# Three dense attentions as one unrolled pipeline of slots, with some scaling moved to GpSimd

## The chip, the cores and the metric

The kernel runs on one core of a Trainium2 chip. The metric is the device time of one launch in microseconds; 2329.51 us is the median of three runs of the kernel before.

## The reference

Four transformer layers, each an attention and a feed-forward part, run on x of 2 x 256 tokens with 512 features; every part starts with a layer norm and adds its result to x. The change touches the attentions of the first three layers, the dense attentions:

```
L0: q = norm(x) Wq, k = ctx Wk, v = ctx Wv (32 heads of 128, 8 key heads; q and k rotated), 512 keys
L1: q = norm(x) Wq, k, v of [ctx, norm(x)]  (16 heads of 96, 4 key heads),  512 + 256 keys
L2: q = norm(x) Wq, k, v of [ctx, norm(x)]  (32 heads of 128, 4 key heads), 512 + 256 keys
x = x + softmax(q k^T * scale [+ mask]) v Wo
```

Float32 accuracy is kept by splitting every operand into a high and a low part (`hi`, `lo`); each product is three matmuls, hi*hi, lo*hi and hi*lo (`passes`, L297).

## The kernel before, in words

A dense attention goes through groups of four query heads: 8 groups in L0, 4 in L1, 8 in L2. One group has the four query heads' projections, the projection of keys and values (in L2 only every second group), 16 tiles of 128 queries by all keys, and the output projection. A tile is: scores on TensorE; the row maximum on VectorE; the exponential with row sum on ScalarE; the reciprocal on VectorE; the scaling, on ScalarE for even and on VectorE for odd tiles (L659, L759); the turn (transposes) on TensorE into a PSUM bank; the high half on ScalarE (L669) and the low half on VectorE (L777). In L1 and L2 the 768 keys of a tile are turned in two pieces, of 512 and 256 columns. Two tiles are a unit, and `attend` multiplies its turned probabilities with the values.

`body` writes one group (two for L2) and `loop` (L410) repeats it in a hardware loop. On TensorE a group is three stretches one after the other: the projections in, then the `PIPE` of 20 steps with the tiles (step i: scores of tile i, turn of tile i-2, at even i attend), then the output projections. The turned pieces p take the PSUM banks `ps_t[p % 3]`, and a turn waits only for the low half of the piece three before it:

```
if p >= 3:
    e.wait_ge(s_tlo, g * (TILES * len(l.pieces)) + (c.piece + p - 2))
```

VectorE in step i does the reciprocal of tile i-1, the low half of the attention's output, the maximum of tile i, the odd scaling, and the low half of tile i-2. In L0 the rotation of q and k (swap of halves on ScalarE L628, products with cosine and sine on VectorE L707 and L708, their sum on GpSimd L477, the halves by L640 and L389) stands ahead of the pipe, and the swap of job r+1 is issued before the sum of job r is waited for. GpSimd else splits the weights that SyncE's queue loads (`split`, L313).

Every engine's queue runs in the order in which it is written, and semaphore counts order the engines among each other. The feed-forward parts and the fourth attention are not touched but for names of PSUM banks.

Of the kernel before, what the change touches and what calls it, by code (L numbers as in the profile page):

```python
# [20 lines left out]
ALU = mybir.AluOpType  # L21
# [7 lines left out]
P = 128  # L29
B, SQ, SK, D = 2, 256, 512, 512  # L30
T = B * SQ
# [35 lines left out]
def program(nc, A, out):  # L67
    ctx = ExitStack()
    with ctx:
# [44 lines left out]
        def attention_space(l):  # L114
# [9 lines left out]
            s.q = [take("q_hi", [P, HG, T], F32R), take("q_lo", [P, HG, T], F32R)]  # L124
# [3 lines left out]
            s.ot = [take("ot_hi", [P, HG, T], F32R), take("ot_lo", [P, HG, T], F32R)]  # L128
# [86 lines left out]
        ps_s = [ctx.enter_context(nc.psum_tensor(f"ps_s{i}", [P, 2, 512], F32)) for i in range(2)]  # L215
# [3 lines left out]
        ring = [ps_s[0][:, 0, :], ps_s[0][:, 1, :], ps_s[1][:, 0, :], ps_s[1][:, 1, :]]  # L219
# [30 lines left out]
        s_go = sem("tile_taken")  # L250
        s_rot = sem("rotation_parts")
        s_swap = sem("halves_swapped")
        s_nat = [sem("even_rows_in"), sem("odd_rows_in")]
# [3 lines left out]
        class Start:  # L257
# [3 lines left out]
            def __init__(self, g, hi, tile, piece, unit, q, kv, o, ra):  # L261
                self.g, self.hi, self.tile, self.piece, self.unit = g, hi, tile, piece, unit
                self.q, self.kv, self.o, self.ra = q, kv, o, ra
        counts = {n: 0 for n in ("g", "hi", "tile", "piece", "unit", "q", "kv", "o", "ra")}
# [8 lines left out]
        def attention_counts(l):  # L273
            n = l.groups
            kv = n // l.kv_every
            phase(l.name, g=kv * l.kv_tiles + n * 8, hi=kv * l.kv_hi + n * HG, tile=n * TILES,
                  piece=n * TILES * len(l.pieces), unit=n * UNITS, q=n, kv=kv, o=n,
                  ra=n * (HG + 2) if l.rope else 0)
# [121 lines left out]

        class Attention:
            def __init__(self, l, A, first_before, free=None):

                self.free = free
                self.l, self.s, self.c = l, SP[l.name], START[l.name]
                self.wkv, self.wq, self.wo = A[l.name + "_wkv"], A[l.name + "_wq"], A[l.name + "_wo"]
                self.first_before = first_before
                self.per = l.kv_every

            def loop(self, e, body):  # L410

                n = self.l.groups // self.per
                with e.Fori(0, n - 1) as i:
                    body(e, i, False)
                body(e, n - 1, True)

            def q_start(self, it, s):

                return it * (self.l.kv_tiles + 8 * self.per) + (self.c.g + (self.l.kv_tiles + 8 * s if s else 0))  # L420

            def o_start(self, it, s):
                return it * (self.l.kv_tiles + 8 * self.per) + (self.c.g + self.l.kv_tiles + 8 * s + HG)

            def hi_start(self, it, s):
                return it * (self.l.kv_hi + HG * self.per) + (self.c.hi + (self.l.kv_hi + HG * s if s else 0))

            def grp(self, it, s):
                return it * self.per + s
# [7 lines left out]
            def sp(self, e):  # L437
                l, c = self.l, self.c

                def body(e, it, last):  # L440
                    for s in range(self.per):
                        g = self.grp(it, s)
                        load(e, "o", None, self.wo[g], ("q", g + (c.q + 1)), parts=l.hd)
                        if s == self.per - 1 and not last:
                            load(e, "kv", None, self.wkv[it + 1], ("kv", it + (c.kv + 1)), cols=2 * l.hd)
                        if not (last and s == self.per - 1):
                            load(e, "q", None, self.wq[g + 1], ("o", g + (c.o + 1)), cols=HG * l.hd)
                self.loop(e, body)
# [12 lines left out]
            def pool(self, e):  # L461
                l, c, sp = self.l, self.c, self.s

                def body(e, it, last):
                    for s in range(self.per):
                        g = self.grp(it, s)
                        q0, o0 = self.q_start(it, s), self.o_start(it, s)
                        more = [("o", g + c.o, q0, p, l.hd, 512) for p in range(4)]
                        if s == self.per - 1 and not last:
                            more += [("kv", it + (c.kv + 1), o0, p, P, 2 * l.hd) for p in range(4)]  # L470
                        if not (last and s == self.per - 1):
                            more += [("q", g + (c.q + 1), o0, p, P, HG * l.hd) for p in range(4)]
                        if l.rope:
                            ra0 = it * (HG + 2) + c.ra
                            for t in range(HG + B):
                                e.wait_ge(s_rot, ra0 * 2 + (2 * t + 2))
                                e.tensor_tensor(sp.ra[:, t % 2, :], sp.ra[:, t % 2, :], sp.rb[:, t % 2, :], ALU.add)\  # L477
                                    .then_inc(s_ra, 1)
                        for job in more:
                            split(e, *job)  # L480
                self.loop(e, body)

            def pe(self, e):
# [3 lines left out]
                def body(e, it, last):  # L488
                    def bank(n, q0):

                        e.wait_ge(g_free, q0 + (n - 3))
                        return ring[n % 4]
                    for s in range(self.per):
                        g = self.grp(it, s)
                        q0, o0 = self.q_start(it, s), self.o_start(it, s)

                        def project_in(o, role, c0, src, lo, first=False):

                            for d in range(DK):
                                if first:  # L500
                                    e.wait_ge(g_free, c.g - 3 + d)
                                    e.wait_ge(w_rdy["q"], g * 8 + (8 * c.q + 2 * d + 2))
                                mm = passes(e, o[0:hd, :], planes(W[role], slice(None), d, slice(c0, c0 + hd)),
                                            planes(src, slice(None), d, slice(lo, lo + 512)), d == 0, d == DK - 1)
                            mm.then_inc(g_full, 1)
                        for hh in range(HG if s == 0 else HG - 1):
                            project_in(bank(hh, q0), "q", hh * hd, xT, 0, hh == 0)
                        if s == 0:

                            e.wait_ge(w_rdy["kv"], it * 8 + (8 * c.kv + 8))  # L510
                            e.wait_ge(s_csplit, DK)
                            for n, (src, lo) in enumerate([(cT, b * SK) for b in range(B)] + ([(xT, 0)] if l.self_keys else []), HG):
                                project_in(bank(n, q0), "kv", 0, src, lo)
# [1327 lines left out]
```

## Time and profile before

| | us |
|---|---|
| median of 3 runs (lowest, highest) | 2329.51 (2327.69, 2330.35) |
| span of the profiled execution | 2328.4 |
| what lies around the span, against the median | 1.1 |
| TensorE matmul busy | 2063.1 (89%) |
| VectorE busy | 1558.6 (67%) |
| ScalarE busy | 1142.4 (49%) |
| GpSimd busy | 901.6 (39%) |
| DMA | 37 GB/s on average |

The profile gives the execution's own time as its span, from the first to the last instruction. A matmul's busy time is its modelled passage through the array, longer than the distance between two starts; where work per matmul is counted below, it is the distance from start to start.

### The profile page before, as it was taken

Reading aid. Unit: us, or ns where it says so; the run is one execution under the profiler, and the core shown is the slowest. Engines: PE = TensorE matmul, PEld = TensorE weight load, DVE = VectorE, ACT = ScalarE, POOL = GpSimd, SP = SyncE. Lnnn points to the kernel's source line nnn. Section 1 sums busy time; section 2 is a strip of 40 time slices with the busy share of each in tenths; the row PEclk is TensorE's granted clock in tenths of the full one; section 3 lists DMA queues with packets and bytes.
Section 4 is the critical chain, followed back from the end, with each engine's and each line's share of the span. In section 5 each row is a group of like instructions: output and inputs, shape, how many; then the busy total and the mean of one; then the engine's idle time right before and its main releaser. Section 6 shows DMA issues by size and latency. Waiting matters only on the chain. (4 is left out here: it accounts for less than half of the span.)

```text
span 2328.4 us, 34351 instructions
## 1 busy us (share of the span) xinstructions
PE 2063.1 (89%) x11612; PEld 1707.9 (73%) x11616; DVE 1558.6 (67%) x3108; ACT 1142.4 (49%) x2338; POOL 901.6 (39%) x850
## 2 busy tenths in 40 slices
PE   5989999899879999987999999999988899996667
PEld 4777777777658788786888888888876677775535
DVE  5677666776657466475764674576564695897999
ACT  3556455565316256351653563555540594782430
POOL 7355533554432322224141233222316674662612
PEclk9999999999989999998999999999999999998889
DMA  3111001110110001001010011001101101002301
GB/s 137 46 45 45 18 27 45 45 36 18 62 30 25 14 22 34 19 12 62 28 37 20 28 37 32 33 19 39 37 28 43 37 1 55 1 19 77 127 18 37
DMA packets 20011, 87.16 MB, mean 37 GB/s; under 512 B 2736, under 2 KB 8624, under 8 KB 11440
## 3 DMA queue, kind: packets, MB, share of 16 engines
q1 hardware_dynamic: 19888, 85.55, 10.6%
q8 instruction: 74, 1.21, 0.2%
q14 instruction: 49, 0.40, 0.1%
HBM read 84.49 MB, written 1.05 MB: 37 GB/s over the span
## 5 line engine op out<-in xcount | busy, mean ns | idle before, releaser
L777 DVE TENSOR_TENSOR l_pt_lo<-ps_t,l_pt_hi 128x512 fp32r<-128x512 f32 (+1 forms) x512 | 283.2, 584 | 87.3 <-ACT l_pt_hi L669 80.1
L323 POOL TENSOR_TENSOR wo_hi<-raw_big,one 128x512 fp32r<-128x512 f32 (+2 forms) x116 | 123.0, 1060 | 489.6 <-PE ps_s L301 460.0
L669 ACT ACTIVATE l_pt_hi<-ps_t 128x512 fp32r<-128x512 f32 (+1 forms) x512 | 243.8, 515 | 108.1 <-PE ps_t L563 103.8
L563 PE MATMUL ps_t<-ident,l_p 128*128 128x128 f32 x1664 | 244.8, 277 | 45.9 <-DVE l_pt_lo L777 29.4
L563 PEld LDWEIGHTS ps_t<-ident,l_p 128*128 128x128 f32 x1664 | 191.9, 141 | 84.3 <-DVE l_pt_lo L777 37.7
L299 PE MATMUL ps_o<-l_pt_hi,l_v_hi 128*128 128x256 f32 (+1 forms) x704 | 211.7, 301 | 14.3 <-DVE l_pt_lo L777 14.3
L323 POOL TENSOR_TENSOR wq_hi<-raw_big,one 128x512 fp32r<-128x512 f32 (+1 forms) x120 | 126.1, 1051 | 199.7 <-PE ps_o L529 98.2
L299 PE MATMUL ps_s<-l_k_hi,l_q_hi 128*128 128x512 f32 (+3 forms) x512 | 195.9, 383 | 7.7 <-DVE l_k_lo L387 3.9
L754 DVE TENSOR_REDUCE nmax<-ps_s 128x1 f32<-128x768 f32 x192 | 183.0, 953 | 28.6 <-PE ps_s L301 28.3
L301 PE MATMUL ps_o<-l_pt_hi,l_v_lo 128*128 128x256 f32 (+1 forms) x704 | 200.0, 284 | 0.0
L300 PE MATMUL ps_o<-l_pt_lo,l_v_hi 128*128 128x256 f32 (+1 forms) x704 | 199.9, 284 | 0.0
L681 ACT ACTIVATE l_p<-ps_s,nmax 128x768 f32<-128x768 f32 x192 | 173.6, 904 | 28.2 <-DVE nmax L754 28.2
L477 POOL TENSOR_TENSOR l_ra<-l_ra,l_rb 128x512 f32<-128x512 f32 x48 | 76.3, 1591 | 271.8 <-DVE l_rb L708 270.7
L300 PE MATMUL ps_s<-l_k_lo,l_q_hi 128*128 128x512 f32 (+3 forms) x512 | 180.8, 353 | 0.0
L301 PE MATMUL ps_s<-l_k_hi,l_q_lo 128*128 128x512 f32 (+3 forms) x512 | 180.6, 353 | 0.0
L1125 POOL TENSOR_TENSOR l_p<-l_p,rinv 128x512 f32<-128x512 f32 x128 | 132.3, 1040 | 84.1 <-DVE rinv L1295 84.1
L299 PE MATMUL ps_s<-xT_hi,wq_hi 128*128 128x512 f32 (+1 forms) x384 | 152.6, 397 | 10.5 <-issue 10.0
L325 POOL TENSOR_TENSOR wq_lo<-raw_big,wq_hi 128x512 fp32r<-128x512 f32 (+1 forms) x120 | 156.4, 1303 | 9.4
L325 POOL TENSOR_TENSOR wo_lo<-raw_big,wo_hi 128x512 fp32r<-128x512 f32 (+2 forms) x116 | 152.0, 1310 | 9.1
L659 ACT ACTIVATE l_p<-l_p,rinv 128x768 f32<-128x768 f32 (+1 forms) x160 | 135.9, 849 | 34.9 <-DVE rinv L735 34.5
L299 PEld LDWEIGHTS ps_o<-l_pt_hi,l_v_hi 128*128 128x128 f32 (+1 forms) x704 | 130.2, 185 | 29.4 <-DVE l_pt_lo L777 21.2
L300 PE MATMUL ps_s<-xT_lo,wq_hi 128*128 128x512 f32 (+1 forms) x384 | 151.1, 394 | 0.0
(309 smaller groups left out, 5552.1 us busy)
## 6 DMA issues: line engine op xcount, KB each, us to landing
raw_big<-in_l_wq SPq DMA_DIRECT2D x18, 1024.0 KB, 5.0
raw_big<-in_l_wo SPq DMA_DIRECT2D x18, 1024.0 KB, 4.9
raw_big<-in_f_w SPq DMA_DIRECT2D x10, 1024.0 KB, 5.0
raw_kv<-in_l_wkv SPq DMA_DIRECT2D x12, 512.0 KB, 5.7
q_nat<-in_f_w1n SPq DMA_DIRECT2D x4, 1024.0 KB, 4.8
q_nat<-in_f_w2n SPq DMA_DIRECT2D x4, 1024.0 KB, 4.8
raw_big<-in_l_wq SPq DMA_DIRECT2D x4, 768.0 KB, 4.7
raw_big<-in_l_wo SPq DMA_DIRECT2D x4, 768.0 KB, 5.5
```

Of the source, the lines that this page charges most:

```text
L299: pe.matmul(o, a[0], b[0], start=start, stop=False)
L300: pe.matmul(o, a[0], b[1], start=False, stop=False)
L301: return pe.matmul(o, a[1], b[0], start=False, stop=stop)
L323: pool.tensor_tensor(hi, w, one[0:parts, 0:1].to_broadcast([parts, cols]), ALU.mult).then_inc(w_rdy[role], 1)
L325: pool.tensor_tensor(lo, w, hi.bitcast(F32), ALU.subtract).then_inc(w_rdy[role], 1)
L563: mm = e.transpose(ps_t[p % 3][:, k * P:(k + 1) * P], sp.p[:, i % 3, (k0 + k) * P:(k0 + k + 1) * P], ident[:, :])
L659: e.activation(pr, pr, ACT.Copy, scale=rinv[:, i - 1:i]).then_inc(s_scl[0], 1)
L669: e.activation(sp.pt[u % 2][0][:, k0:k0 + nk, qt * P:(qt + 1) * P], ps_t[p % 3][:, 0:nk * P].rearrange("p (k q) -> p k q", q=P), ACT.Copy) ...
L681: e.activation(sp.p[:, i % 3, :], src, ACT.Exp, bias=nmax[:, i:i + 1], scale=-1.0 if l.rope else 1.0, accum_out=rsum[:, i:i + 1]).then_inc ...
L754: e.tensor_reduce(nmax[:, i:i + 1], ps_flat(i)[:, 0:l.keys], AX.X, ALU.max, negate=True).then_inc(s_max, 1)
L777: e.tensor_tensor(pt[1], ps_t[p % 3][:, 0:nk * P].rearrange("p (k q) -> p k q", q=P), pt[0].bitcast(F32), ALU.subtract).then_inc(s_tlo, 1)
L1125: e.tensor_tensor(l3p[:, i % 4, :], l3p[:, i % 4, :], rinv[:, i % TILES:i % TILES + 1].to_broadcast([P, SK]), ALU.mult).then_inc(s3["scl"], 1)
```

## The change

The hardware loops go; the attention is written out as one sequence of slots over all its tiles (`N` = 128, 64, 128), with six or eight slots ahead of tile 0 that hold one whole projection each and four behind. In slot k TensorE does scores of tile k, then parts of projections (a part is three matmuls, a quarter of a job), turned values, the turn of tile k-2, and at even k attend. `ORDER` spreads a group's jobs evenly over its 16 slots: q of the next group, o (the output projection) of the group before, k and v of the next; a capital letter is the part of the keys that comes from x (256 columns). L1 has 16 jobs a group, one per slot; L0 and L2 have 12, three parts per slot. Group 0 has no o jobs and the last group no q jobs and no k0, v0.

q has two buffers, and the attention's output is written into the q it came from. The projections use two PSUM banks in turn, ring[3] and ps_t[2]; the turned pieces therefore have two banks (before three), and attend one (before two in L0). In L1 and L2 the scores of odd and even tiles share a bank for their x keys. The odd tiles of L1 and L2 are scaled on GpSimd, between weight splits assigned to slots; in L0 they stay on VectorE.

```
 ORDER = {
   "l0": ["k1 o0 o1 v1 o2 o3 q0 k0 q1 v0 q2 q3"],
   "l1": ["k1 K1 o0 v1 V1 o1 o2 o3 q0 k0 K0 q1 v0 V0 q2 q3"],
   "l2": ["k1 K1 o0 v1 V1 o1 o2 o3 q0 q1 q2 q3", "o0 o1 o2 o3 q0 q1 k0 K0 q2 v0 V0 q3"]}
 FIRST = {"l0": "q0 q1 q2 q3 k0 v0", "l1": "q0 k0 K0 q1 v0 V0 q2 q3", "l2": "q0 k0 K0 q1 v0 V0 q2 q3"}
   # TensorE
+  def take_turn_bank(p):
+      if p >= 2:
+          e.wait_ge(s_tlo, c.piece + p - 1)
+      return ps_t[p % 2]
+  for k in self.slots:
+      if 0 <= k < self.N: scores(k)
+      for j, part in self.parts.get(k, ()): project(j, part)
+      for j in self.values.get(k, ()): turn_values(j)
+      if 0 <= k - 2 < self.N: turn(k - 2)
+      if self.unit_at(k) is not None: attend(self.unit_at(k))
   # inside scores(k)
+      if k >= 2: e.wait_ge(s_max if l.rope else s_exp, c.tile + k - 1)
...
+      if l.self_keys and k >= 1: e.wait_ge(s_exp, c.tile + k)     # ahead of the x keys
   # ScalarE, slot k
+      turned_hi(k - 3)                       # high halves of tile k-3
+      # high half of attend's output (odd k)
+      for j in self.ended.get(k - 1, ()):    # rotated jobs only
+          e.wait_ge(s_ra, j.rope + 1); e.activation(qk_tile hi, sp.ra)
+      e.wait_ge(s_max, ...); e.activation(... ACT.Exp ...)
+      # high half of turned values
+      for j in self.ended.get(k, ()):        # wait g_full: swap of halves (L0), or high half of q/k
+      if k % 2 == 0: e.wait_ge(s_rec, ...); e.activation(pr, pr, ACT.Copy, scale=rinv)
   # VectorE, slot k
+      largest(k)
+      turned_lo(k - 3)
+      # low half of attend's output (odd k)
+      # low half of the q/k rotated in slot k-1
+      # reciprocal of tile k
+      # low half of turned values
+      for j in self.ended.get(k, ()):        # rotate(j), or low half of q/k, or copy of v / x += o
+      if k % 2 == 1 and l.rope: tensor_scalar(pr, pr, rinv)
   # GpSimd, L1 and L2
+      if i % 2:
+          e.wait_ge(s_rec, c.tile + k + 1)
+          e.tensor_scalar(pr, pr, rinv[:, i:i + 1], None, ALU.mult).then_inc(s_scl[1], 1)
+      if 2 <= i < 6: next_q(g, i - 2)
+      if kv_at <= i < kv_at + 2: next_kv(g, 2 * (i - kv_at)); next_kv(g, 2 * (i - kv_at) + 1)
+      if o_at <= i < o_at + 4: own_o(g, i - o_at)
```

(A comment stands for a call whose operation is as in the kernel before.) SyncE's queue issues the same loads in the order q of the next group, kv, o.

## Rows read from the trace of the kernel before

**Rows 1.** Busy time by stretch: L0, L1, L2, then two groups of L2.
```profile
17.00:616.00 599.00, 540.63 (x2891) 441.50 (x2889) 396.77 (x861) 331.13 (x680) 285.32 (x248) 0.98 0.10 36
680.00:1041.00 361.00, 347.07 (x2080) 291.70 (x2079) 210.05 (x401) 178.01 (x364) 87.52 (x97) 0.98 0.09 24
1080.00:1731.00 651.00, 623.20 (x3808) 549.86 (x3808) 400.16 (x754) 340.51 (x700) 169.18 (x163) 0.99 0.09 31
1346.59:1506.96 160.37, 154.37 (x950) 136.02 (x949) 98.70 (x185) 84.45 (x174) 42.60 (x40) 1.00 0.09 31
```

**Rows 2.** Waits of the weight loads in L1: total us, times, longest.
```profile
PEld ps_t L563 <- DVE l_pt_lo L777: 11.3, 8, 1.8
PEld ps_o L529 <- DVE xn L766: 2.7, 4, 0.7
```

**Rows 3.** The same in L2.
```profile
PEld ps_t L563 <- DVE l_pt_lo L777: 26.4, 26, 2.0
...
PEld ps_s L299 <- DVE l_q_lo L389: 2.4, 4, 0.6
```

**Rows 4.** Timeline of TensorE in L2: start, duration, operation.
```profile
1366.37 0.82 PE L563 MATMUL ps_t<-ident,l_p 128*128 128x128 f32 x6
...
1371.61 0.40 PE L299 MATMUL ps_s<-l_k_hi,l_q_hi 128*128 128x512 f32 x1
1371.84 0.40 PE L300 MATMUL ps_s<-l_k_lo,l_q_hi 128*128 128x512 f32 x1
...
1372.66 0.60 PE L563 MATMUL ps_t<-ident,l_p 128*128 128x128 f32 x4
```

**Rows 5.** Timeline of L2: VectorE, and the turn that waits for it.
```profile
1368.29 1.02 DVE L777 TENSOR_TENSOR l_pt_lo<-ps_t,l_pt_hi 128x512 fp32r<-128x512 f32 x2 [0.30 <-ACT l_pt_hi L669]
...
1369.03 0.44 PE L563 MATMUL ps_t<-ident,l_p 128*128 128x128 f32 x2 [0.36 <-DVE l_pt_lo L777]
...
1369.54 0.96 DVE L754 TENSOR_REDUCE nmax<-ps_s 128x1 f32<-128x768 f32 x1
...
1370.41 0.61 DVE L759 TENSOR_SCALAR l_p<-l_p,rinv 128x768 f32<-128x768 f32 x1
...
1372.86 0.96 DVE L754 TENSOR_REDUCE nmax<-ps_s 128x1 f32<-128x768 f32 x1 [0.21 <-PE ps_s L301]
```

**Rows 6.** Timeline of L0: exponential, low half, attend.
```profile
216.12 0.71 ACT L681 ACTIVATE l_p<-l_p,nmax 128x512 f32<-128x512 f32 x1
...
216.26 0.69 DVE L777 TENSOR_TENSOR l_pt_lo<-ps_t,l_pt_hi 128x512 fp32r<-128x512 f32 x1 [0.19 <-ACT l_pt_hi L669]
...
217.01 0.39 PE L299 MATMUL ps_o<-l_pt_hi,l_v_hi 128*128 128x256 f32 x1 [0.28 <-DVE l_pt_lo L777]
```

**Rows 7.** Timeline of L0: one rotation.
```profile
181.97 1.21 ACT L628 ACTIVATE l_rb<-ps_s 64x512 f32<-64x512 f32 x2 [1.51 <-PE ps_s L301]
...
183.21 0.69 DVE L707 TENSOR_TENSOR l_ra<-ps_s,l_cos 128x512 f32<-128x512 f32 x1 [1.43 <-ACT l_rb L628]
...
184.58 1.67 POOL L477 TENSOR_TENSOR l_ra<-l_ra,l_rb 128x512 f32<-128x512 f32 x1 [1.43 <-DVE l_rb L708]
...
186.28 0.63 ACT L640 ACTIVATE l_q_hi<-l_ra 128x512 fp32r<-128x512 f32 x1 [0.38 <-POOL l_ra L477]
```

**Rows 8.** Timeline of L0: rotations at its start, first scores, last projection.
```profile
37.74 0.63 ACT L640 ACTIVATE l_q_hi<-l_ra 128x512 fp32r<-128x512 f32 x1 [11.86 <-POOL l_ra L477]
...
52.59 0.50 PE L299 MATMUL ps_s<-l_k_hi,l_q_hi 128*128 128x512 f32 x1 [0.48 <-DVE l_k_lo L387]
...
611.38 0.39 PE L299 MATMUL ps_s<-wo_hi,l_ot_hi 128*128 128x512 f32 x1
...
612.51 0.39 PE L301 MATMUL ps_s<-wo_hi,l_ot_lo 128*128 128x512 f32 x1
```

**Rows 9.** Page, costliest groups: scaling of 512 columns on GpSimd, fourth attention.
```profile
L1125 POOL TENSOR_TENSOR l_p<-l_p,rinv 128x512 f32<-128x512 f32 x128 | 132.3, 1040 | 84.1 <-DVE rinv L1295 84.1
```

**Rows 10.** Page, DMA queues: instructions.
```profile
q8 instruction: 74, 1.21, 0.2%
```

More of the change, by code:

```diff
@@ L123, in take @@
                 return a
-            s.q = [take("q_hi", [P, HG, T], F32R), take("q_lo", [P, HG, T], F32R)]
+            s.q = [[take(f"q{i}_{n}", [P, HG, T], F32R) for n in ("hi", "lo")] for i in range(2)]
             s.k = [take("k_hi", [P, B, l.keys], F32R), take("k_lo", [P, B, l.keys], F32R)]
@@ L438, in sp @@
                 l, c = self.l, self.c
[L440 to L448, printed above, removed]
+                for g in range(l.groups):
+                    before = self.raw_before(g)
+                    if g + 1 < l.groups:
+                        load(e, "q", None, self.wq[g + 1], before, cols=HG * l.hd)
+                        before = ("q", c.q + g + 2)
+                    kv = g // l.kv_every
+                    if g % l.kv_every == 0 and kv + 1 < self.kvs:
+                        load(e, "kv", None, self.wkv[kv + 1], ("kv", c.kv + kv + 1), cols=2 * l.hd)
+                    load(e, "o", None, self.wo[g], before, parts=l.hd)
             def pool_first(self, e):
@@ L462, in pool @@
                 l, c, sp = self.l, self.c, self.s
[L464 to L480, printed above, removed]
@@ L481, in pool, with next_q, next_kv @@
-                self.loop(e, body)
+                def next_q(g, piece):
+                    if g + 1 < l.groups:
+                        split(e, "q", c.q + g + 1, self.full(self.find["q", g, 3, False]), piece, cols=HG * l.hd)
+                def next_kv(g, piece):
+                    kv = g // l.kv_every
+                    if g % l.kv_every == 0 and kv + 1 < self.kvs:
+                        split(e, "kv", c.kv + kv + 1, self.full(self.find["v", kv, 1, l.self_keys]), piece, cols=2 * l.hd)
@@ L617, in act @@
+                for k in self.slots:
+                    if 0 <= k < self.N:
+                        scores(k)
+                    for j, part in self.parts.get(k, ()):
+                        project(j, part)
+                    for j in self.values.get(k, ()):
+                        turn_values(j)
+                    if 0 <= k - 2 < self.N:
+                        turn(k - 2)
+                    if self.unit_at(k) is not None:
+                        attend(self.unit_at(k))
             def act(self, e):
@@ new lines, in project_out @@
+                def project_out(j):
+                    e.wait_ge(g_full, self.full(j))
+                    if j.kind == "v":
+                        if j.stage >= 4:
+                            old = [v for v in self.jobs if v.stage == j.stage - 4][0]
+                            e.wait_ge(s_T, c.piece + self.v_piece[old.n] + 1)
+                        e.tensor_copy(xn[0:hd, j.stage % 4, 0:j.width], self.bank(j)[0:hd, 0:j.width]).then_inc(g_free, 1)
+                        return
+                    t = j.i
+                    if j.g:
+                        e.wait_ge(g_free, self.full(self.find["o", j.g - 1, t, False]))
+                    e.tensor_tensor(x[:, t, :], self.bank(j), x[:, t, :], ALU.add).then_inc(g_free, 1)
+                    if j.g == l.groups - 1 and t < TT - 1:
+                        e.wait_ge(g_free, self.full(j))
+                        e.bn_stats(st[:, t, :], x[:, t, :])
```

655 lines of the change are left out of this document (340 added, 315 removed), and 3 rows, old and new, of the table ORDER.

## The prediction

> **What bounds the kernel now.** First the busy time by stretch [rows 1]: in the three dense attentions (599, 361 and 651 us) TensorE's matmuls are busy for 540.6, 347.1 and 623.2 us, at a granted clock of 0.98 to 0.99, while VectorE has 397, 210 and 400. TensorE bounds all three. A busy time overstates a pipelined matmul, so I count from start to start. In the timeline of L2 [rows 4] a matmul of 512 columns takes 1371.84 - 1371.61 = 0.23 us (0.227 over the five steps between the last two starts of [rows 8]), one of 256 columns 0.12, the scores of a tile with 768 keys 1372.66 - 1371.61 = 1.05, six transposes 0.65 and four 0.44 (0.109 each; the six start at 1366.37 and take 0.82 to their modelled end). In these units the work is: L0 a group, twelve jobs of 12 x 0.227 = 2.72, 16 scores of 0.70, 16 turns of 0.44, 8 attends of 12 x 0.12 = 1.44, turned values 0.9: 63.3 us. L1 84, two groups of L2 together 150.8. In all 505, 337 and 602 us, so that 94, 24 and 49 us are not work. That is all that an ideal pipeline could win, 167 us.
>
> Second the waits of the weight loads, which show a gap as it is from start to start: L1 11.3 us behind the low half of the turned pieces and 2.7 behind the values [rows 2]; L2 26.4 and 2.4 [rows 3] and again 2.7 behind the values (word for word the row of [rows 2]). The rest of L1 and L2 (10 and 17 us) is the end of the attention up to the next norm and rounding of my units; it stays.
>
> **The change, L1 and L2.** What goes: 14.0 and 31.5 us of waits [rows 2, 3]. What comes is one wait for every slot. With two banks in place of three, the first piece of tile k-2 may be turned only when the low half of the first piece of tile k-3 is done, and VectorE does that in the same slot k, behind the maximum of tile k, which waits for the scores of slot k. The rows price it [rows 5, 4]: scores end (1372.66) to maximum 0.20; maximum to VectorE's next operation 1370.41 - 1369.54 = 0.87; start of a low half to the turn that it releases 1369.03 - 1368.29 = 0.74. So the turn of slot k starts no earlier than 1.81 us after its scores, that is 2.86 into the slot. Between them lie only the projection parts, and what decides is whether they last 1.81:
> - Full slots do: three parts 2.04 (L2), a job 2.72 (L1). No stall. VectorE's last operation, the low half of a job, ends at 4.6 (1.05 + 2.04 + 0.2 + 0.64 for the high half + 0.61), in an odd slot of 3.74 that is 0.9 into the next, whose maximum starts at 1.25.
> - A slot with a K or V job has 1.44 in L1, 1.40 in L2: 0.4 us.
> - A slot without a job: 1.81.
> - Where values are turned too, the second piece of tile k-2 waits for their low half, which on VectorE stands behind the reciprocal and on ScalarE behind the exponential: values turned to 3.3, high half 3.5 to 4.1, low half visible at 4.87. That is 1.5 us in a slot with a short job, 0.6 behind a full one, 2.3 where there is no job.
>
> L1: group 0 lacks its four o jobs (three plain 1.81, one 2.4 with values: 7.8) and has 0.4 + 1.5 + 1.5 + 0.6 for the others: 11.8. Groups 1 and 2 have 0.4 x 2 + 1.5 x 2 + 0.6 x 2 = 4.9 each. Group 3 has eight slots without a job, 14.5, and 2.5 for its first half: 17.0. The last turns, without a maximum between, wait for high and low half in turn: 2. Sum 40.6.
> L2: group 0 lacks 16 of 48 parts: 12.7. The six groups between: three short slots at 0.4, values 1.55 and 0.6: 3.4 each, 20.4. Group 7 lacks 32 parts: ten slots at 1.81 and one at 1.1, 19.2. End 2. Sum 54.3.
> Net: L1 40.6 - 14.0 = +26.6; L2 54.3 - 31.5 = +22.8.
>
> **The scaling on GpSimd.** The nearest row is the fourth attention's, 1.04 us for 512 columns [rows 9]; 768 columns of one operand lie between 1.04 and, by width, 1.56; I take 1.56, the cautious one. The reciprocal is there at 3.5 in slot k, the turn starts at 3.1 in slot k+2, in all 9.2 us later. Beside it stand at most two pieces of split, 2.3 each, queued behind it and not ahead of it. If it took twice 1.56 the turn would still find it done. VectorE is relieved of 0.61 to 1.7 us every second tile, but it is not what bounds. Zero, from 0 to +3 us.
>
> **L0.** Its tiles have one piece, so the two banks cost nothing: low half of tile k-3 is needed by attend, at 0.70 + 2.04 + 0.44 = 3.18 in an even slot; without a delay it is there at 0.9 + 0.65 + 0.74 = 2.3 (low half to attend 217.01 - 216.26 = 0.75 [rows 6]). The delay comes from the rotation. In slot k ScalarE waits for the sum of the job that ended in slot k-1 ahead of the exponential, and swaps the halves of slot k's job behind it; VectorE rotates behind that, ahead of the next maximum. So successive rotated jobs form a circle: swap 1.24, the two products 1.37, sum 1.67, high half 0.65 [rows 7], exponential 0.71 [rows 6]: 5.6 us and, with the odd scaling that meets the sum, 6, against 3.9 for a slot. I walk it from slot 9, whose job q0 ends with its first part (start 0, odd slot 3.18, even 4.62):
> - slot 9: swap to 3.6, rotation to 4.85, odd scaling to 5.4, sum to 7.1. Slot 10: maximum 5.4, low half 6.8, attend wanted 6.36: 0.4 late, ends 8.24.
> - slot 10's k0: ScalarE 7.1 high half, 7.7 exponential, 8.4 swap; rotation to 10.9, sum to 12.7. Slot 11's q1: exponential 13.4, swap to 15.3, rotation and scaling to 17.1.
> - slot 12 (from 11.4): attend wanted 14.6; maximum 17.1, low half 18.5: 3.9 late.
> - slots 14 and 15 do the same in a chain of two: attend of the next slot 0 is 2.65 late; k1 in slot 1 makes slot 2's 0.8 late.
> Sum 7.8, a group of 71.1 us. Six groups so: 426.6. Group 0, without o jobs and first attends, 55 (48.5 of work); group 7, without rotation in its second half, 55 (46.9 of work, 8 of waits); the end, four o jobs, two turns and attends, 16.
> Ahead of them the start: before, the first high half came at 37.74 and the first scores at 52.59 [rows 8], since the swap of the next job was issued early. Now four more jobs take 4.85 + 0.05 each (1.24 + 1.37 + 1.67 + 0.65), k0's high half is at 57.3 to 58.0 and the scores start at 58.8: 6.2 later.
> New end: 58.8 + 55 + 426.6 + 55 + 16 = 611.4, against 612.51 + 0.2 [rows 8]: -1.3. What L0 wins by laying projections beside tiles it loses in the circle. Bounds: -55 if the circle is covered, +15 if every odd scaling waits for GpSimd for another microsecond (one at each of four chains in eight groups would be 32, of which half is covered).
>
> **Unrolling.** The instruction queue moved 74 blocks, 1.21 MB [rows 10], and also the fourth attention, which is straight-line code before, draws on it. Their share, 0.2% of 16 engines' span, is 74.5 us, 1.0 a block. I take 0 for the further blocks, since they can come while TensorE works, and as a bound as many again, none hidden: +74. By this page alone the unrolled attentions would fetch every block, which is the case of rival 3.
>
> **Sum.** -1.3 + 26.6 + 22.8 = +48.1; the span 2328.4 becomes 2376.5, and with the 1.1 us between span and median 2378 us, 2.1% slower. Nothing behind the attentions changes in kind; SyncE's loads are issued at least two slots ahead of their splits.
>
> **Rivals.**
> 1. The circle of L0 does not hold TensorE up, since ScalarE and VectorE have caught up by each attend: the 54.5 us of its stalls (46.8 + 4.3 + 3.4) go, 2378 - 54 = 2324. For it: in a slot without a rotated job nothing is late, and the circle holds for at most three. Against: the attend behind it is in order. It decides once the stalls are under 1 us a group.
> 2. The other side: the pipeline runs at TensorE's pace throughout, because the low halves are never the last to arrive. The place is the turn in slots without a full job; the price is 40.6 + 54.3 on top of rival 1: 2324 - 95 = 2229. It is faster from the point where half of the 95 and half of the 54 go. For it: 167 us of room. Against: VectorE's order puts the maximum of tile k ahead of the low half of k-3, in every slot, and 12 of L1's 64 and about 17 of L2's 128 slots have no job.
> 3. Every further block of instructions holds TensorE for its 1.0 us [rows 10]: 2378 + 74 = 2452. For it: the loops are gone. Against: the fourth attention and the norms are written out already, and no wait of [rows 2, 3] lies with instructions.
>
> **How the numbers follow.** Forecast 0.70 (own range 2345 to 2402: the waits of L1 and L2 a third smaller or larger, -32 to +20 with L0's +15 and GpSimd's 3 in part), rival 1 0.13, rival 2 0.13 (2229 to 2300, mostly part of it), rival 3 0.04. The forecast and rival 3 are slower but for 0.01 at the forecast's lower end. This kernel's measurement tells 0.2%, 4.7 us, from no change. Faster: rival 2 and more than half of rival 1, 0.21. Within 0.2%: 0.06, the rest of rival 1 and that 0.01. Slower: 0.73. The range leaves out most of rival 2 and rival 3: 2318 to 2402.
>
> **What would show it.** After the change TensorE's waits in L1 and L2 are the turn's, behind `l_pt_lo`, and lie in the first group, the last group and at values; groups between run at about 89 us (L1) and 79 (L2), that is, no slower than the 89.4 and 80.2 before. L0's groups run at 71 with attend late in slots 12 and 0. First scores of L0 at 58.8. Wrong would be: a turn in slots without a job that starts less than 1.8 us behind the scores; L0's groups under 68 us; GpSimd as the one a turn waits for.

## The result

| | median us | runs | to before |
|---|---|---|---|
| before | 2329.4 | 2327.7 to 2330.4 | |
| changed | 2453.7 | 2452.1 to 2456.4 | 1.0535 [1.052, 1.055] |

The change made the kernel 124 us slower, 5.3%. The prediction said slower, 2378 us, with 2402 as its upper end: the direction was right, the size less than half. All times here are of fast runs; one of experiment 11's six, 2440.4 us in the slow state with a granted clock of 0.82 in place of 0.96, is left out. From norm to norm, and between them only the attention, the three stages went from 606.0, 366.1 and 655.4 us to 624.5, 398.2 and 730.0: +18.5, +32.2 and +74.6, where -1.3, +26.6 and +22.8 were predicted. The stages behind them kept their times within 2 us.

The busy time by stretch of the changed kernel: L0, L1, L2 from norm to norm, then an even and an odd group of L2 (columns as in [rows 1]).

```profile
8.90:633.36 624.46, 550.38 (x2896) 463.66 (x2896) 389.86 (x865) 337.87 (x680) 282.75 (x253) 0.95 0.11 40
691.37:1089.60 398.23, 358.34 (x2176) 302.89 (x2176) 195.55 (x385) 181.96 (x372) 160.64 (x133) 0.96 0.08 22
1123.60:1853.60 730.00, 637.56 (x3904) 556.63 (x3904) 356.77 (x705) 347.29 (x708) 311.48 (x230) 0.96 0.08 28
...
1323.80:1403.30 79.50, 75.77 (x482) 66.61 (x480) 42.99 (x87) 42.97 (x88) 39.06 (x31) 1.00 0.04 14
1403.30:1496.80 93.50, 81.14 (x492) 70.55 (x493) 43.24 (x87) 43.01 (x89) 38.08 (x26) 0.96 0.11 40
```

The reader is to see the last two rows: the odd group is 14 us longer, while VectorE, ScalarE and GpSimd are as busy as in the even one. A pair of groups had 160.4 us before [rows 1] and has 173.0 now. TensorE's waits in L2 say for what. These are the rows of its matmuls (engine, what it ran, what released it; total us, times, longest), where [rows 3] has those of the weight loads. Before, the row of the turn was

```profile
PE ps_t L563 <- DVE l_pt_lo L777: 20.0, 23, 1.7
```

and now four rows are

```profile
PE ps_t L695 <- DVE l_pt_lo L809: 32.4, 35, 1.8
PE ps_s L298 <- POOL wq_lo L324: 19.3, 3, 6.4
PE ps_s L298 <- issue: 13.3, 4, 3.3
PE ps_t L695 <- DVE l_v_lo L871: 10.1, 14, 1.0
```

Rows one and four are the waits that the prediction counted. Row two is one that it did not have: in each of the three full odd groups q0 waits 6.4 us for the last piece of its weights' split. GpSimd's timeline in one such group (start, duration, operation) shows why that piece is late:

```profile
1429.56 1.29 POOL L324 TENSOR_TENSOR wq_lo<-raw_big,wq_hi 128x512 fp32r<-128x512 f32 x1
1434.84 2.20 POOL L582 TENSOR_SCALAR l_p<-l_p,rinv 128x768 f32<-128x768 f32 x1 [3.98 <-DVE rinv L868]
1437.01 1.04 POOL L322 TENSOR_TENSOR wq_hi<-raw_big,one 128x512 fp32r<-128x512 f32 x1
1438.12 1.26 POOL L324 TENSOR_TENSOR wq_lo<-raw_big,wq_hi 128x512 fp32r<-128x512 f32 x1
```

GpSimd is free at 1430.85, but the next thing in its queue is the scaling of tile 5, and that waits for the reciprocal, thus for the scores of slot 5. Only then comes the fourth piece, in the very slot in which q0 starts. The wait has a second price. The busy time by stretch up to its end, at 1439.5, through the 5.3 us that follow, and on:

```profile
1403.30:1439.50 36.20, 26.57 (x162) 22.96 (x163) 14.62 (x30) 14.05 (x28) 17.90 (x13) 0.98 0.08 30
1439.50:1444.80 5.30, 5.27 (x16) 4.34 (x17) 0.00 (x0) 0.87 (x2) 0.00 (x0) 0.51 0.50 198
1444.80:1496.80 52.00, 49.29 (x316) 43.26 (x315) 28.63 (x57) 28.08 (x59) 20.19 (x13) 1.00 0.08 31
```

The granted clock is 0.51, near the lower of the two levels, 1.2 GHz, right after the wait.

A full odd group is 94.7 us in the mean, 15.9 above the predicted 78.8 (half of 150.8, and 3.4 of waits). Slot by slot: q0's wait 6.4 and 2.5 more for the matmuls behind it; o0's wait in slot 0 for its own weights, whose last piece is placed in slot 15, 3.3 to 3.5 (row three of the waits, once in each odd group; the profile names no releaser, but the last piece of that split ends at 1405.50 and o0 starts at 1405.60); in two of the three groups the matmuls behind this wait ran at the lower clock too, and these groups are 1.6 and 2.0 us longer than the third; o2's in slot 3 for the low half of its attend's output, 1.1.

### The profile page after: what moved, and what is told of

Read it like the earlier page. It is cut to its first block and busy times, and to the rows that moved or that the text cites. A ratio compares the mean times of both kernels' runs of the same rounds, so it can differ in the third digit from the quotient of the medians.

```text
span 2452.1 us, 32169 instructions
## 1 busy us (share of the span) xinstructions
PE 2096.9 (86%) x11804; PEld 1745.1 (71%) x11808; DVE 1481.8 (60%) x3036; ACT 1159.7 (47%) x2354; POOL 1098.8 (45%) x946
## 5 line engine op out<-in xcount | busy, mean ns | idle before, releaser
L582 POOL TENSOR_SCALAR l_p<-l_p,rinv 128x768 f32<-128x768 f32 x96 | 211.6, 2204 | 633.5 <-DVE rinv L868 633.5
L298 PE MATMUL ps_o<-l_pt_hi,l_v_hi 128*128 128x256 f32 (+1 forms) x832 | 255.1, 307 | 42.0 <-DVE l_pt_lo L809 41.2
L695 PEld LDWEIGHTS ps_t<-ident,l_p 128*128 128x128 f32 x1664 | 197.9, 142 | 127.0 <-issue 70.9
L300 PE MATMUL ps_o<-l_pt_hi,l_v_lo 128*128 128x256 f32 (+1 forms) x832 | 241.8, 291 | 0.0
L299 PE MATMUL ps_o<-l_pt_lo,l_v_hi 128*128 128x256 f32 (+1 forms) x832 | 241.5, 290 | 0.0
L298 PEld LDWEIGHTS ps_o<-l_pt_hi,l_v_hi 128*128 128x128 f32 (+1 forms) x832 | 159.4, 192 | 49.4 <-DVE l_pt_lo L809 48.8
L597 POOL TENSOR_TENSOR l_ra<-l_ra,l_rb 128x512 f32<-128x512 f32 x48 | 66.5, 1386 | 253.0 <-DVE l_ra L834 253.0
L322 POOL TENSOR_TENSOR wq_hi<-raw_big,one 128x512 fp32r<-128x512 f32 (+1 forms) x120 | 125.4, 1045 | 102.8 <-PE ps_s L300 97.8
L299 PEld LDWEIGHTS ps_o<-l_pt_lo,l_v_hi 128*128 128x128 f32 (+1 forms) x832 | 160.2, 193 | 0.1
L300 PEld LDWEIGHTS ps_o<-l_pt_hi,l_v_lo 128*128 128x128 f32 (+1 forms) x832 | 160.1, 192 | 0.0
```

Of the source, the lines that this page charges most:

```text
L298: pe.matmul(o, a[0], b[0], start=start, stop=False)
L299: pe.matmul(o, a[0], b[1], start=False, stop=False)
L300: return pe.matmul(o, a[1], b[0], start=False, stop=stop)
L322: pool.tensor_tensor(hi, w, one[0:parts, 0:1].to_broadcast([parts, cols]), ALU.mult).then_inc(w_rdy[role], 1)
L582: e.tensor_scalar(pr, pr, rinv[:, i:i + 1], None, ALU.mult).then_inc(s_scl[1], 1)
L695: mm = e.transpose(o[:, kk * P:(kk + 1) * P], sp.p[:, k % 3, at:at + P], ident[:, :])
```

## Experiments

**1. Splits placed earlier, in L2.**

```diff
-                        o_at = 8 if g % l.kv_every else 12
+                        o_at = 8 if g % l.kv_every else 11 if l.kv_every == 2 else 12
...
-                        if 2 <= i < 6:
+                        if g % l.kv_every:
+                            for piece in {2: (0, 1), 3: (2,), 4: (3,)}.get(i, ()):
+                                next_q(g, piece)
+                        elif 2 <= i < 6:
                             next_q(g, i - 2)
```

> L2 alone: in the odd groups GpSimd splits the next q weights in slots 2, 2, 3, 4 in place of 2 to 5, and in the even groups its own o weights in slots 11 to 14 in place of 12 to 15. Theory (late weight splits): the odd groups of L2 are 95.1, 93.5 and 95.4 us because q0 waits for its last split, which is placed in the very slot where it is needed, behind a scaling that waits for that slot's scores, and because the clock then falls to half. With the splits earlier both go, and these groups come to the 79 us of the even ones; the 3.5 us wait of o0 in slot 0 goes too: about -48 us, 2405. Rival (the order of the odd groups is itself slow: key and value jobs in other slots): the wait for the weights goes but the groups stay above 90 us, less than 20 us gained.

Measured: 2405.3 us (2404.6 to 2409.6), -48.4. The same odd and even groups by stretch:

```profile
1308.90:1388.40 79.50, 76.79 (x488) 67.63 (x487) 42.96 (x87) 42.97 (x89) 41.21 (x32) 1.00 0.08 27
1388.40:1469.20 80.80, 77.16 (x488) 67.63 (x487) 43.22 (x87) 42.91 (x89) 36.01 (x24) 1.00 0.09 33
```

93.5 became 80.8 with the clock at 1.00, no wait for `wq_lo` and none without a releaser is left, and the turn's waits kept their row to the digit (32.4 us, 35 times). The order of the odd groups costs 1.3 us, not 14. L2 is now 683.4 us, 28 above before: close to the predicted +22.8.

**2. Odd tiles scaled on VectorE again, splits where they were.**

```diff
-                        if i % 2:
-                            e.wait_ge(s_rec, c.tile + k + 1)
...
-                            e.tensor_scalar(pr, pr, rinv[:, i:i + 1], None, ALU.mult).then_inc(s_scl[1], 1)
...
-                    if 0 <= k < self.N and k % 2 == 1 and l.rope:
+                    if 0 <= k < self.N and k % 2 == 1:
```

> L1 and L2: the odd tiles are scaled on VectorE again, at the end of the slot as in L0; the weight splits stay in their slots. Theory (the splits are late because a scaling that waits for the slot's scores is queued ahead of them): GpSimd is free to run ahead, no TensorE wait for weights is left, and L2's odd groups come to 79 to 82 us: about -45 us, with 0 to +10 back from VectorE's longer slots, so 2410 to 2420. Rival (it is the slot that is wrong, not what is queued ahead: GpSimd is limited by its own 2.2 us of splits and by the loads): the waits stay, and the time is within 10 us of 2453.

Measured: 2409.3 us (2407.1 to 2414.2), -44.4. L2's odd groups are 81.7 us with the splits in the same slots. So it is not the slot alone that was wrong, but the waiting instruction ahead of the splits: experiments 1 and 2 remove nearly the same from a group (14 and 13 us in the mean), once by moving the splits out from behind it, once by taking it away. Experiment 2 also takes the 2.2 us of the scaling off GpSimd; experiment 1 leaves them there, so that this load was not what made the weights late.

**3. Low half ahead of the largest value.**

```diff
-                    if 0 <= k < self.N:
-                        largest(k)
                     if 0 <= k - 3 < self.N:
                         turned_lo(k - 3)
+                    if 0 <= k < self.N:
+                        largest(k)
```

> All three attentions: VectorE takes the low half of the turned tile of three slots ago before the largest value of this slot's tile, not behind it. Theory (the turn of a slot without a job waits for a low half that is queued behind the reduction of this slot's scores, 1.9 us each): the low half runs beside the scores, the turn finds its bank free, and the waits of slots without a job go: about 25 slots x 1.9 in L1 and L2 and part of L0's attend waits: -45 us, between -30 and -60. Rival (the wait is ScalarE's: the high half comes late, so the low half waits anyway, and the reduction and all that follows it move back): within 10 us of 2453, or slower.

Measured: 2404.3 us (2402.7 to 2405.8), -49.4: L1 -17.8, L2 -25.9, L0 only -3.3. A slot without a job in the changed kernel (timeline of all engines, cut to the chain: last scores, maximum, low half, turn):

```profile
1034.11 0.28 PE L300 MATMUL ps_s<-l_k_hi,l_q_lo 96*128 96x256 f32 x1
1034.43 0.96 DVE L801 TENSOR_REDUCE nmax<-ps_s 128x1 f32<-128x768 f32 x1 [3.54 <-PE ps_s L300]
1035.30 1.01 DVE L809 TENSOR_TENSOR l_pt_lo<-ps_t,l_pt_hi 128x512 fp32r<-128x512 f32 x2
...
1036.13 0.85 PE L695 MATMUL ps_t<-ident,l_p 128*128 128x128 f32 x6 [1.74 <-DVE l_pt_lo L809]
```

and in this version:

```profile
1017.92 0.28 PE L300 MATMUL ps_s<-l_k_hi,l_q_lo 96*128 96x256 f32 x1
1017.95 1.02 DVE L809 TENSOR_TENSOR l_pt_lo<-ps_t,l_pt_hi 128x512 fp32r<-128x512 f32 x2 [1.49 <-ACT l_pt_hi L743]
...
1018.79 0.84 PE L695 MATMUL ps_t<-ident,l_p 128*128 128x128 f32 x6 [0.59 <-DVE l_pt_lo L809]
1018.89 0.95 DVE L801 TENSOR_REDUCE nmax<-ps_s 128x1 f32<-128x768 f32 x1
```

The wait was VectorE's order, as the prediction had it: from the last scores' start to the turn 2.02 us, less the 0.12 that this matmul takes, is 1.90; 1.81 was forecast. It falls to 0.75 by the same count, not to zero: the low half now waits for ScalarE's high half (1.49 of idle time ahead of it).

**4. The first cut of L0's circle.** High and low half of a rotated operand move behind the scaling, to the end of the slot.

```diff
 # ScalarE; the same move for operand_lo on VectorE
-                    for j in self.ended.get(k - 1, ()):
-                        if j.rope is not None:
-                            e.wait_ge(s_ra, j.rope + 1)
...
                         e.activation(pr, pr, ACT.Copy, scale=rinv[:, k % TILES:k % TILES + 1]).then_inc(s_scl[0], 1)
+                    for j in self.ended.get(k - 1, ()):
+                        if j.rope is not None:
+                            e.wait_ge(s_ra, j.rope + 1)
...
```

> L0 alone: the high and low half of a rotated operand are taken at the end of the slot behind that of its job, not ahead of exp and of the reciprocal; VectorE waits for the low half of two rotated jobs ago before it writes that buffer again. Theory (circle: exp waits for the rotated sum on GpSimd, and so the chain of every slot that follows a rotated job is late; about 9 us a group in slots 12, 0, 2 and 10): groups of 71 to 72 come to 63 to 65 us, stage L0 -50 us, between -35 and -60. Rival (L0 is bound by what ScalarE and VectorE have to do, not by the order): L0 within 15 us of before.

Measured: 2451.0 us (2448.4 to 2453.6), -2.7, which the spread of the runs nearly covers; stage L0 is 1.0 us shorter. The time is the rival's and this theory fell, but experiment 7 will show that the rival's reason is not the right one either. Attend still waits 2.9 us in slot 12 and 2.5 in slot 0. The start times of VectorE's largest values in slots 9 to 12 told where to look next: in the changed kernel 4.4, 5.1 and 5.7 us apart, here 4.4, 4.7 and 6.1. With the halves gone from the front, a second chain is nearly as long: largest value, exponential, two swaps, two products, odd scaling, and only then the next largest value. Part of what was gained on it went into a slow operation; VectorE, then GpSimd, at the end of slot 11's work in this version:

```profile
317.72 1.75 DVE L816 TENSOR_TENSOR l_k_lo<-l_ra,l_k_hi 128x512 fp32r<-128x512 f32 x1
319.40 0.68 DVE L797 CUSTOM_DVE_ANT_0 l_p<-ps_s,l_mask 128x512 f32<-128x512 f32 x1
```

```profile
317.49 1.43 POOL L597 TENSOR_TENSOR l_ra<-l_ra,l_rb 128x512 f32<-128x512 f32 x1 [2.95 <-DVE l_ra L836]
318.88 1.49 POOL L322 TENSOR_TENSOR wo_hi<-raw_big,one 128x512 fp32r<-128x512 f32 x1
```

The low half of k0, started 0.2 us into GpSimd's sum, took 1.75 us, against 0.69 in the changed kernel, where GpSimd was idle.

**5. Experiments 1 and 3 together.**

> The earlier splits of L2 and the low half ahead of the largest value, together. Theory (two separate losses: weights that come late in full slots of L2, and the turn's bank in slots without a job): the gains of 48 and 49 us add up, 2356, between 2350 and 2365; the odd groups of L2 at 79 to 80 us, no TensorE wait for weights left. Rival (they are the same time seen twice): 2380 or more.

Measured: 2363.2 us (2360.3 to 2365.2), -90.5 of 97.8. The two losses are separate but for 7 us: L2 came down by 66.9, not by 46.6 + 25.9. Of the 5.6 us between, 3.4 are in the three full odd groups, where the low half first wins 3.5 us a group while the weights are late and 2.4 when they are not; q0's wait itself is hardly shorter in experiment 3 (18.9 us against 19.3), and what makes this difference was not tried.

**6. GpSimd's scaling as tensor_tensor.**

```diff
-                            e.tensor_scalar(pr, pr, rinv[:, i:i + 1], None, ALU.mult).then_inc(s_scl[1], 1)
+                            e.tensor_tensor(pr, pr, rinv[:, i:i + 1].to_broadcast([P, l.keys]), ALU.mult).then_inc(s_scl[1], 1)
```

> The odd tiles of L1 and L2 are scaled on GpSimd by tensor_tensor with the reciprocal broadcast along the row, not by tensor_scalar. Theory (the 2.20 us of an odd scaling are the price of the instruction's form; tensor_tensor in L3 took 1.04 us for 512 columns): 1.56 us each for 768, and every split queued behind one comes 0.64 us earlier: the wait of q0 in L2's odd groups shortens from 6.6 to 6.0 us, and the time by 2 to 8 us. Rival (2.20 us is what 768 columns cost on GpSimd in either form): no change of the instruction, within 3 us of 2453.

Measured: 2447.1 us (2441.5 to 2451.1), -6.5. The costliest groups of the changed kernel and of this one, the scaling alone (columns as in [rows 9]):

```profile
L582 POOL TENSOR_SCALAR l_p<-l_p,rinv 128x768 f32<-128x768 f32 x96 | 211.6, 2204 | 633.5 <-DVE rinv L868 633.5
```

```profile
L582 POOL TENSOR_TENSOR l_p<-l_p,rinv 128x768 f32<-128x768 f32 x96 | 141.0, 1468 | 699.7 <-DVE rinv L868 699.7
```

The form of the instruction costs 0.74 us; by width alone the 1.04 of [rows 9] gave 1.56, and tensor_tensor stays below that. In L2, q0's waits fell from 19.3 to 17.0 us and o0's from 13.3 to 10.2, and the stage from 730.0 to 721.3. The profiled run is the slowest of the four (2451.1), and its L1 is 4.2 us longer, which was not followed up; so the -6.5 of the median is good to some us only.

**7. The second cut of L0's circle.** The swaps leave the chain.

```diff
-        FIRST = {"l0": "q0 q1 q2 q3 k0 v0",
+        FIRST = {"l0": "k0 q0 q1 q2 q3 v0",
 # GpSimd: the sum one slot later
-                    for j in self.ended.get(k, ()):
+                    for j in self.ended.get(k - 1, ()):
...
 # ScalarE, ahead of exp: the swaps of the job that ended in slot k-1, in place of its high half
-                            e.wait_ge(s_ra, j.rope + 1)
...
+                            e.wait_ge(g_free, self.full(j))
...
 # ScalarE, behind exp: the high half of the job that ended in slot k-2
+                    for j in self.ended.get(k - 2, ()):
...
 # VectorE: sine product of the job that ended in slot k-1, low half of k-2's, cosine product of k's
-                            operand_lo(j, sp.ra[:, j.rope % 2, :], s_qk)
+                            rotate(j, 1)
...
-                            rotate(j)
+                            rotate(j, 0)
```

TensorE waits, before it reuses a projection bank, for the swaps too.

> L0 alone, the circle cut at another place: VectorE takes the cosine product at the end of the job's slot; ScalarE's two half-swaps, the sine product and GpSimd's sum follow in the next slot, the high and low half in the one after; k0 is projected first. Theory of the revised circle (largest value 0.75, exp 0.92, two swaps 1.2, two products 1.4 and the odd tile's scaling 0.5 follow one another before VectorE can begin the next slot's largest value: 4.4 to 5.3 us in a slot, where TensorE needs 3.1 and 4.6, so three rotated jobs in successive slots, 9 to 11, push the chain back until attend waits in slot 12, and 14 and 15 in slot 0): with the swaps out of this chain the waits of slots 12 and 0 fall from 7.2 us to under 2, groups of 72 us come to 64 to 66, L0 -35 to -50 us. Rival A (the engines' own load in these slots, 3.9 us on VectorE and ScalarE alike, is what binds): groups at 69 or more, less than 15 us gained. Rival B (the bank of the projections is freed later and TensorE waits for that): as many us lost in slots 2 and 10 as are gained.

Measured: 2402.2 us (2400.5 to 2408.3), -51.5; stage L0 571.3 us in place of 624.5. One of its groups by stretch, and TensorE's waits in it:

```profile
182.20:246.80 64.60, 64.31 (x361) 54.54 (x361) 49.00 (x108) 41.59 (x84) 33.62 (x30) 1.00 0.12 43
```

```profile
PEld ps_s L298 <- issue: 0.9, 2, 0.6
PEld ps_o L298 <- DVE l_pt_lo L811: 0.3, 1, 0.3
```

72.0 became 64.6, with 63.3 of work. Of the stage's 53.2 us, 40.8 are in groups 1 to 6, 5.6 in group 0, 4.5 at the end, and 2.3 in the start, where k0 is now the first job. VectorE and ScalarE have the same operations as before: the order was the bound, not their load (rival A), and the bank is not late (rival B).

**8 and 9. All three edits; then with the low half first in L1 and L2 alone.**

```diff
-                    if 0 <= k < self.N:
+                    if 0 <= k < self.N and l.rope:
                         largest(k)
                     if 0 <= k - 3 < self.N:
                         turned_lo(k - 3)
+                    if 0 <= k < self.N and not l.rope:
+                        largest(k)
```

> Earlier splits, low half first, and the swap in the next slot, together. Theory (three separate losses): 2356 less 35 to 50, so 2306 to 2321, which would be faster than the kernel before (2328.5). Rival (L0 does not gain, as when the halves alone were moved): 2350 to 2356.

> As the version with all three edits, but the low half goes ahead of the largest value in L1 and L2 alone; in L0 the largest value stays first. Theory (in L0 each tile's largest value, exp and scaling make the chain that paces the slot, and a low half that waits for ScalarE's high half in front of it delays it: its L0 stage was 584.5 us against 571.3 with the swap alone): 2329.2 less 13, 2316, between 2312 and 2320; L0 groups back at 64.6. Rival (the 13 us belong to something else in that build): within 3 us of 2329.

Measured: the first 2329.2 us (2326.7 to 2333.0), 0.9999 [0.9990, 1.0009] of before; the second 2317.3 us (2315.6 to 2319.0), 0.9951 [0.9938, 0.9964]. The first missed its expected 2306 to 2321. Over experiment 5 (2363.2, which was expected at 2356) it gains 34 us, where the swap alone had gained 51.5: its L0 groups are 66.1 us, not 64.6, and the stage 584.5 against 571.3, since in L0 a low half that waits ahead of the largest value delays it. The second has the groups at 64.6 and is 0.5% faster than before, the best of the versions. Its three stages:

```profile
8.87:580.29 571.42, 526.56 (x2896) 443.13 (x2896) 402.90 (x865) 338.56 (x680) 288.11 (x253) 0.98 0.12 43
638.43:1019.16 380.73, 349.28 (x2176) 296.72 (x2176) 199.92 (x385) 178.08 (x372) 160.92 (x133) 0.98 0.08 23
1052.85:1713.69 660.84, 619.90 (x3904) 547.34 (x3904) 364.16 (x705) 342.38 (x708) 312.19 (x229) 0.99 0.09 31
```

Against before that is -34.6, +14.7 and +5.5 us. The new structure wins in L0 and still loses in L1, whose last group has eight slots without a job.

**10. The same with the odd scaling on VectorE.**

> The version just described, with the odd tiles of L1 and L2 scaled on VectorE again. It asks what the move to GpSimd is worth once no weights are late. Theory (full slots are TensorE's, and in slots without a job the turn waits for the previous tile's halves, not for the scaling): within 5 us of 2316 either way; L1 3 us shorter as before, L2 up to 4 longer. Rival (VectorE's extra 0.7 us in odd slots lengthens the slots without a job): 8 us or more slower than that version.

Measured: 2340.6 us (2339.6 to 2343.1), 1.0055 [1.0042, 1.0068] of before and 23.3 above version 9: the rival held, and its price was larger than said. Two places carry it. In a slot without a job VectorE takes the scaling ahead of the low half (VectorE in a late slot of L1):

```profile
976.29 0.16 DVE L875 RECIPROCAL rinv<-rsum 128x1 f32<-128x1 f32 x1 [0.73 <-ACT l_p L765]
976.49 0.96 DVE L894 TENSOR_SCALAR l_p<-l_p,rinv 128x768 f32<-128x768 f32 x1
977.37 1.01 DVE L810 TENSOR_TENSOR l_pt_lo<-ps_t,l_pt_hi 128x512 fp32r<-128x512 f32 x2
```

Version 9 starts the same low half 0.48 us after the reciprocal's start, this one 1.08. And in a slot with values the turn's second piece starts 2.3 us late where it was 1.7, after which the clock falls (this version; the second row is the attend behind it):

```profile
1270.05:1275.50 5.45, 3.59 (x26) 3.04 (x24) 3.83 (x8) 3.05 (x8) 3.13 (x5) 1.00 0.00 0
1275.50:1279.57 4.07, 3.90 (x21) 3.90 (x22) 1.46 (x4) 1.03 (x3) 2.12 (x4) 0.59 0.01 4
```

Version 9's same slot lasts 7.5 us, not 9.5, at 1.00 throughout. So in this slot half a microsecond more of waiting cost two. L2 is 21.5 us longer and L1 4.8. In L2 12.4 of them are in the six steady groups (80.2 and 80.7 us in the main in place of 78.0 and 78.3), 3.0 in group 0 and the rest in the last group and the end; how they divide between the two places was not counted.

**11. Version 9 with tensor_tensor on GpSimd.**

> The same version, with GpSimd's scaling done by tensor_tensor (1.47 us in place of 2.20). Theory (with the splits placed early nobody waits for GpSimd): within 3 us of 2316. Rival (the scaling ends last before a turn in slots without a job, or the splits queued behind it still matter): 4 us or more faster.

Measured: 2316.4 us (2315.9 to 2319.6), 0.9954 [0.9941, 0.9967] of before: the same as version 9. Once no split is queued late behind the scaling, its 0.74 us are worth nothing.

## Why the prediction was right in direction and wrong in size

**L2, the step that failed.** "Beside it stand at most two pieces of split, 2.3 each, queued behind it and not ahead of it", and "SyncE's loads are issued at least two slots ahead of their splits". The term for the scaling was "Zero, from 0 to +3 us". The first sentence asked whether the splits delay the scaling, and never the reverse: a scaling that waits for a reciprocal holds back the splits behind it, and the fourth piece stands in slot 5, where q0 of the odd groups starts. Nor were the slots of the splits laid beside the slots of their first use for the odd order of L2. The predicted +22.8 became +74.6; with the splits moved (experiment 1) it is +28.0. That is shown: 46.6 us of the miss of 51.8 in L2 are this, out of 75.7 in all; L0 adds 19.8 and L1 5.6.

**L2 and L1 otherwise.** The price of a slot without a job was 1.81 forecast, 1.90 measured; even groups of L2 78.8 forecast, 79.5 measured; groups of L1 89 forecast, 89.0 measured. The sum of the new stalls in L1 was 40.6 forecast and is 45.6 from start to start: group 0 has 16.9 where 11.8 was said. Its slot 6 comes behind three waits in a row, and by stretch (scores and wait, then turn and attend) it looks like this:

```profile
745.79:749.80 4.01, 2.27 (x9) 1.72 (x7) 1.70 (x3) 1.39 (x3) 3.85 (x5) 0.50 0.00 0
749.80:754.95 5.15, 5.15 (x24) 5.15 (x25) 0.35 (x2) 1.98 (x5) 3.59 (x7) 0.50 0.57 153
```

At a granted clock of 0.50 its matmuls took 3.3 us more; the forecast priced waits, not what follows them. The 5 us more of stalls are most of the 5.6 between +26.6 and +32.2. Experiment 3 shows the mechanism of the waits.

**L0.** Start, forecast 58.8, measured 57.08; it is k0 whose low half ends last, as said. Groups 1 to 6 together 426.6 forecast, 428.2 measured, attend late by 2.9 in slot 12 (3.9 forecast) and 2.1 in slot 0 (2.65). That the sum fits is partly luck. The waits of a group came to 5.4 to 5.7 us, not 7.8; the first of the six groups had the clock at 1.00 and took 69.4 us, the others had it at 0.95 to 0.98 and took 70.8 to 72.1, a price that the forecast did not have. The mechanism was right in part. The walk put the sum and the high half (1.67 + 0.65) on the chain, and there they are: in slot 11 ScalarE idles for the sum ahead of k0's high half and of the exponential (the changed kernel):

```profile
316.68 0.63 ACT L756 ACTIVATE l_k_hi<-l_ra 128x512 fp32r<-128x512 f32 x1 [1.24 <-POOL l_ra L597]
317.22 0.71 ACT L761 ACTIVATE l_p<-l_p,nmax 128x512 f32<-128x512 f32 x1
```

But experiment 4 took them off it and won 1.0 us in the stage, since a second chain is nearly as long, from largest value over exponential, swaps and products to the next largest value. Experiment 7, which took the swaps and the sine product off that one as well, won 53. The two mis-sized terms are the ends. Slots 0 to 15 of group 0 took 66.1 us, not 55: 48.75 of work, and 17.4 of stalls where the forecast had 6.5. Some 10.7 of these are waits and the rest goes with a granted clock of 0.91. That its short slots have too little to cover turn and attend is argued; experiment 7 takes 5.6 us off this group too, so the rotations have a part. Group 7 and the end took 79.1, not 71. Together +19.2, less 1.7 at the start and with 1.6 in between: the last projection ends at 630.4, not 611.4.

**The scaling on GpSimd.** 1.56 taken, 1.04 to 1.56 as the bounds, 2.20 measured: outside. A range by width from a different form of instruction was no bound. With the splits placed early its length does not matter, as said (experiment 11); queued ahead of late splits, 0.74 us of it cost 5.4 us of waits in L2 (experiment 6). Nor was the relief of VectorE worth nothing: in the order of version 9 it is 23 us (experiment 10).

**The rivals.** Rival 3 gave 2452, the time measured, and is wrong nonetheless. The instruction queue moved more blocks than [rows 10], as it supposed:

```profile
q8 instruction: 96, 1.57, 0.3%
```

But they are 22 more, not 74, and experiment 9, with the same unrolled code, ran at 2317; full slots run without a stall, and the excess lies at waits with a named releaser, but for o0's 13.3 us, which went when the splits moved (experiment 1). Straight code did fetch more blocks; that fetching them holds TensorE up is what did not come. A number that fits is no evidence for its mechanism. Rivals 1 and 2 did not come about in this kernel. Rival 1's size did, once its condition was made: it asked for stalls under 1 us a group and 54 us, and experiment 7 has 1.3 and 51.5.

## What to carry to other kernels

When an instruction that waits goes onto a queue, look at what stands behind it as well as at what it stands behind: for each piece of work placed by slot on that engine, write down the slot in which it is first used, for every order of the jobs that occurs, and leave a slot between. In an in-order pipeline of several engines, list every closed chain from one slot's first operation to the next one's; cutting one that ties with another wins nothing, which a single small experiment tells. A software pipeline is full only in the middle: its first and last group need their own sum of stalls. And price behind a wait what the matmuls after it cost at the lower clock; whether it falls could not be told from the length of the wait here, as the rows below show.

## What the runs showed of the hardware

- GpSimd scales 768 columns by a column of factors in 2.20 us as tensor_scalar and in 1.47 as tensor_tensor with the factor broadcast; VectorE takes 0.61 alone, and up to 1.70 beside GpSimd's splits (experiment 10).
- A VectorE operation with both inputs in SBUF was held up by a GpSimd operation that started before it. The low half of a rotated operand took 0.69 us where GpSimd was idle. Started inside a GpSimd operation it took what was left of that one and 0.55 more: 0.85 with 0.30 left of a split (changed kernel), 1.10 with 0.55 left of a split and 1.75 with 1.20 left of a rotation's sum (experiment 4). Where VectorE started first, the sum beside it cost it nothing, and the sum took 1.74 us in place of 1.30 (experiment 4, VectorE, then GpSimd):

```profile
312.70 0.69 DVE L818 SCALAR_TENSOR_TENSOR l_q_lo<-l_ra,l_q_hi 128x512 fp32r<-128x512 f32 x1
```

```profile
312.80 1.74 POOL L597 TENSOR_TENSOR l_ra<-l_ra,l_rb 128x512 f32<-128x512 f32 x1 [2.95 <-DVE l_ra L836]
```

  The low halves of turned pieces, which have one input in PSUM, stayed at 0.69 or less beside any of them.
- The granted clock was 0.51 for the 5.3 us after q0's wait of 6.4, and 0.59 for 4 us after the turn was 2.3 late in a slot with values, while in the same slot 1.7 left it at 1.00. Equal waits were followed by either level. After o0's wait of 3.3 us in the three full odd groups of L2 it was

```profile
1230.99:1235.90 4.91, 4.91 (x14) 3.93 (x15) 0.00 (x0) 0.00 (x0) 0.00 (x0) 0.50 0.59 214
1405.60:1410.50 4.90, 4.90 (x33) 4.45 (x34) 0.00 (x0) 0.87 (x2) 0.00 (x0) 1.00 0.60 214
1578.60:1583.50 4.90, 4.90 (x14) 3.92 (x15) 0.00 (x0) 0.00 (x0) 0.00 (x0) 0.50 0.57 214
```

  and in L1's last group four waits of 1.9 passed at 1.00, while behind the fifth, which ends at 1054.9, it fell to the lower level for 7 us:

```profile
1033.18:1055.46 22.28, 13.58 (x98) 12.04 (x97) 10.95 (x23) 11.24 (x23) 6.70 (x4) 1.00 0.00 0
1055.46:1062.50 7.04, 5.30 (x24) 4.76 (x23) 2.05 (x4) 3.56 (x7) 6.74 (x5) 0.52 0.01 2
```
